# Convolution ahead of the context's norm, one scan quarter's stacks moved to transfers, later entry of two attention loops' last rows, and four more products ahead of the router's transposes

## What is computed

```
x = ln(x + mamba_block(x))            # ln, projection, depthwise conv of 3, selective scan, gate, small FFN
x = ln(x + cross_attention_0(x, ctx)) # 16 heads of 64, rotary keys, clipped logits
x = ln(x + moe_0(x))                  # 8 experts, top 2, GELU
x = ln(x + self_attention_1(x))       # 16 heads of 8, rotary                    ("a" below)
x = ln(x + cross_attention_1(x, ctx)) # 16 heads of 8, with a mask               ("x" below)
x = ln(x + moe_1(x))                  # 32 experts of 64, grouped top 6 of sigmoid scores, relu^2, one shared expert
# the scan of the first block, per channel d and state n:
#   delta = softplus(xc @ dt_w + dt_b);  h = exp(delta * A) * h + (delta * xc) * B;  y = sum_n h * C + D * xc
```

## Time and profile before

| | us |
|---|---|
| median of 3 runs | 506.44 (505.37 to 507.49) |
| profiled execution, its own time | 506.76 |
| its span in the profile | 505.0 |
| time outside the span | 1.76 |
| PE busy | 423.4 (84%) |
| DVE busy | 310.4 (61%) |
| ACT busy | 203.9 (40%) |
| chain that ended last: on PE | 56% |
| chain that ended last: on DVE | 27% |

### The profile page before, as it was taken

How to read it: one execution, slowest core, us unless ns; L and a number is a source line. 1 busy time by engine, 2 the same in 40 slices (tenths; PEclk the granted TensorE clock), 3 DMA queues, 4 the chain that set the end, 5 groups by cost and what they waited for, 6 DMA issues and landing times.

```text
span 505.0 us, 7196 instructions
## 1 busy us (share of the span) xinstructions
PE 423.4 (84%) x2724; PEld 256.2 (51%) x2732; DVE 310.4 (61%) x733; ACT 203.9 (40%) x259; POOL 142.2 (28%) x133
## 2 busy tenths in 40 slices
PE   0538989999999998799998867896768999979794
PEld 0207645444454466657668554445324455564493
DVE  4669976866777764325113689734996773237564
ACT  0565633233333331143333397670334445517400
POOL 3204656787767765101203000002000000014301
PEclk9868999999999999899999899899789999979898
DMA  8601000000023110600431500000000000010000
GB/s 299 246 19 55 1 2 1 1 1 1 0 75 135 42 43 14 228 16 25 92 46 29 74 13 2 3 2 1 1 1 2 1 3 3 1 31 2 0 1 21
DMA packets 7360, 19.37 MB, mean 38 GB/s; under 512 B 1751, under 2 KB 3127, under 8 KB 6807
## 3 DMA queue, kind: packets, MB, share of 16 engines
q1 hardware_dynamic: 7324, 18.91, 12.6%
HBM read 17.26 MB, written 1.15 MB: 36 GB/s over the span
## 4 chain that ended last, share of the span: by engine, by line
PE 56%; DVE 27%; issue 6%; POOL 5%; ACT 5%; DMA 1%; another core or an unknown queue 0%; DVEq 0%; POOLq 0%
PE ps L1228 53%; DVE ps L1081 4%; DVE mx_a L1085 2%; DVE ps L889 2%; DVE big L894 2%; POOL rstd L498 2%; POOL big L561 1%; ACT big L724 1%; DVE stats L797 1%; PE ps L1240 1%; PE ps L1601 1%; DVE big L966 1%; POOL big L568 1%; DVE normed L807 1%; DVE mid L825 1%
## 5 line engine op out<-in xcount | busy, mean ns | idle before, releaser
L1228 PE MATMUL ps<-big,late 128*32 128x256 f32 (+4 forms) x792 | 100.3, 381 | 11.3 <-DVE mx_x L1081 3.8
L1228 PE MATMUL ps<-late,big 128*128 128x128 f32 (+1 forms) x448 | 64.9, 277 | 3.4 <-DVE mx_x L1081 1.8
L750 ACT ACTIVATE big<-ps 128x1024 f32<-128x1024 f32 x48 | 48.9, 1024 | 39.3 <-PE ps L1228 39.0
L1228 PEld LDWEIGHTS ps<-big,late 128*32 128x32 f32 (+3 forms) x800 | 37.9, 115 | 51.1 <-issue 22.6
L496 POOL TENSOR_SCALAR vareps<-meanvar 128x4 f32<-128x4 f32 (+1 forms) x9 | 2.1, 231 | 212.1 <-DVE meanvar L800 212.1
L688 ACT ACTIVATE big<-ps 128x1024 f32<-128x1024 f32 x32 | 32.8, 1025 | 65.2 <-PE ps L1228 58.9
L1228 PEld LDWEIGHTS ps<-late,big 128*128 128x128 f32 (+1 forms) x448 | 45.0, 152 | 27.3 <-issue 20.6
L1081 DVE CUSTOM_DVE_ANT_0 ps<-ps,big 128x512 f32<-128x512 f32 x64 | 42.6, 716 | 10.5 <-PE ps L1228 7.5
L561 POOL TENSOR_TENSOR big<-big 128x512 f32<-128x512 f32 x32 | 41.0, 1283 | 28.1 <-DVE big L966 28.1
L966 DVE TENSOR_SCALAR big<-big 128x1024 f32<-128x1024 f32 x32 | 27.6, 863 | 33.3 <-ACT big L688 33.3
L1228 PE MATMUL ps<-ctx_r,attn_w 128*128 128x512 f32 x64 | 32.6, 618 | 0.7 <-ACT late L655 0.7
(11 more groups left out here) (246 smaller groups left out, 692.7 us busy)
## 6 DMA issues: line engine op xcount, KB each, us to landing
attn_w<-in_w_x SPq DMA_DIRECT2D x1, 2560.0 KB, 13.1
big<-parts_kx SPq DMA_DIRECT2D x18, 128.0 KB
late<-in_w_up SPq DMA_DIRECT2D x1, 2048.0 KB, 7.5
late<-in_w_dn SPq DMA_DIRECT2D x4, 512.0 KB, 3.8
attn_w<-in_w_up SPq DMA_DIRECT2D x1, 1024.0 KB, 7.1
attn_w<-in_w_dn SPq DMA_DIRECT2D x1, 1024.0 KB, 9.1
parts_kx<-ctx_r SPq DMA_DIRECT2D x1, 768.0 KB, 3.2
rowv<-in_rowv SPq DMA_DIRECT2D x1, 576.0 KB, 3.9
```

The lines of the kernel that those rows point to most:

```text
L750: nc.scalar.activation(ex1[:, n % 3, :].rearrange("p (r n) -> p r n", r=2), ps[:, 2 * (n % 2):2 * (n % 2) + 2, :], ACT.Exp, scale=scale).t ...
L1228: return nc.tensor.matmul(o, lhsT, rhs, start=start, stop=stop, skip_group_check=shared)
```

## The change

- ACT loads its first table before it waits for xT. DVE takes the context's statistics, then the convolution, then normalises the context. PE transposes the context behind the products for delta, B and C. POOL's residual sum waits for the context's norm.
- |z| is read by ACT straight from PSUM. ACT loads the exp table behind Silu, and computes A (`negA`) behind the context's evictions.
- PE gets 20, 10 and 20 idle products in the opening.
- Quarter 1's stacks are made by 6 further DMAs in place of DVE's 6 copies. The DMAs are issued by quarter (1, 2, 3), delta then delta*x in each. `ORDER`, `SUMMED` and the places of `y_of` (steps 7, 9, 14) follow.
- In both attentions the last two rows of the first stretch go to banks 6 and 7, and logits(0) waits for all rows but these two. `AHEAD["x"]` goes from 29 to 24. The spreads stand earlier. The exp table is loaded ahead of "a".
- `EARLY` goes from 12 to 16.

```diff
-        ORDER = ([(q, i) for two in ((0, 1), (2, 3)) for i in range(2) for q in two]
+        ORDER = ([(0, 0), (0, 1), (1, 0), (1, 1), (2, 0), (3, 0), (2, 1), (3, 1)]
                  + [(q, i) for i in (2, 3) for q in range(4)])
-        SUMMED = ((0, 1, 4, 5), (2, 3, 6, 7), (8, 9, 10, 11), (12, 13, 14, 15))
+        SUMMED = ((0, 2, 4, 5), (1, 3, 6, 7), (8, 9, 10, 11), (12, 13, 14, 15))
-        AHEAD = {"a": 24, "x": 29}
+        AHEAD = {"a": 24, "x": 24}
...
-            return ([(None, s, i % 4) for i, s in enumerate(first_slots(L))]
+            first = first_slots(L)
+            banks = [i % 4 for i in range(len(first) - 2)] + [6, 7]
+            return ([(None, s, bank) for s, bank in zip(first, banks)]
                     + [(n, s, 6 + i % 2) for i, (n, s) in enumerate(later)])
...  SP
-            for kind, parts in enumerate(("delta_parts", "dx_parts")):
-                for q in (2, 3):
+            for q in (1, 2, 3):
+                for kind, parts in enumerate(("delta_parts", "dx_parts")):
                     for i in range(PARTS):
...
-                                     ).then_inc(S["late_quads"], 16)
+                                     ).then_inc(S["second_quads" if q == 1 else "late_quads"], 16)
...  POOL
-            pool.wait_ge(ld["x"], 16)
+            pool.wait_ge(norm_out, normed_tiles("ctx"))
...
-                    pool.wait_ge(S["y_ps"], 1 if s < 10 else 2)
+                    pool.wait_ge(S["y_ps"], 1 if s == 8 else 2)
...  ACT
+            act.wait_ge(consts, 1)
+            set_table(ACT.Identity)
             to_cols(xT[:], 0, "xT_ps", "xT_done", v("ln_g"), v("ln_b"), 1)
...
+            set_table(ACT.Exp)
+            act.wait_ge(S["dt_ps"], 1)
+            nc.scalar.activation(dtmp[:, 0, :], ps[:, 3, :], ACT.Abs, bias=v("dt_b")
+                                 ).then_inc(S["z_done"], 1)
             act.wait_ge(S["z_done"], 1)
-            link(nc.scalar.activation(dtmp[:, 0, :], cv[:, 1, :], ACT.Abs))
...
+            set_table(ACT.Exp)
             act.wait_ge(ld["sel_s"], 32)
...  DVE: quad() is called for quarter 0 alone
-            quad(1, 0, "dx_quads")
-            quad(0, 1, "delta_quads")
-            quad(1, 1, "dx_quads")
+            quad(1)
...  PE
             pe.wait_ge(ld["ident"], 16)
+            idle_work(3, 20)
...
+            idle_work(3, 10)
             pe.wait_ge(S["xc_done"], 1)
...
+            idle_work(2, 20)
...
-                if s in (8, 10, 14):
+                if s in (7, 9, 14):
...
-                        return range(4) if m < 0 else [4 + m // 2] if m % 2 and 4 + m // 2 < 16 else []
-                    return [0] if m < 0 else [1 + m // 4] if m % 4 == 1 and 1 + m // 4 < 8 else []
+                        return range(5) if m < 0 else [5 + m // 2] if m % 2 and 5 + m // 2 < 16 else []
+                    return [0] if m < 0 else [1 + m // 3] if m % 3 == 1 and 1 + m // 3 < 8 else []
...
+                    if slot == ("row", AHEAD[L] - 2):
+                        pe.wait_ge(S[f"{L}_spread"], len(SPREADS[L]))
...
-                pe.wait_ge(S[f"{L}_redmax"], AHEAD[L])
-                pe.wait_ge(S[f"{L}_spread"], len(SPREADS[L]))
+                pe.wait_ge(S[f"{L}_redmax"], AHEAD[L] - 2)
...
-            EARLY = 12
+            EARLY = 16
```

More of the change, by code:

```diff
@@ L364, in before_in_bank @@
             at = [s for _, s, _ in placed].index(slot)
-            same = [s for n, s, bank in placed[:at]
-                    if bank == placed[at][2] and (n is None) == (placed[at][0] is None)]
+            same = [s for n, s, bank in placed[:at] if bank == placed[at][2]]
             return same[-1] if same else None
@@ L641, in _ @@
                         v("ctx_g"), v("ctx_b"), i + 1)
+            link(nc.scalar.activation(nA[:, 0, :], vec[:, VEC["A_log"][0]:VEC["A_log"][0] + NG],
+                                      ACT.Exp))
+            nc.scalar.mul(nA[:, 1, :], nA[:, 0, :], -1.0).then_inc(S["negA"], 1)
             act.wait_ge(S["negA"], 1)
@@ L843, in _ @@
             dve.wait_ge(ld["cx"], 16)
-            layernorm("ctx", cx, cx)
+            k_ctx = NORMS.index("ctx")
+            for j in range(NC_TILES):
+                ins = nc.vector.bn_stats(stats[:, j, :], cx[:, j, :])
+            link(ins)
+            for j in range(NC_TILES):
+                ins = nc.vector.bn_aggr(meanvar[:, k_ctx, j, :], stats[:, j, :])
+            ins.then_inc(norm_var, 1)
+            dve.wait_ge(norm_var, k_ctx + 1)
             dve.wait_ge(ld["vec"], 16)
@@ L853, in _ @@
                                            ALU.mult, ALU.add).then_inc(S["conv_done"], 1)
+            dve.wait_ge(norm_rstd, k_ctx + 1)
+            for j in range(NC_TILES):
+                nc.vector.tensor_scalar(cx[:, j, :], cx[:, j, :], meanvar[:, k_ctx, j, 0:1],
+                                        rstd[:, k_ctx, j:j + 1], ALU.subtract, ALU.mult
+                                        ).then_inc(norm_out, 1)
+            dve.wait_ge(norm_out, normed_tiles("ctx"))
             dve.wait_ge(ld["rope0"], 16)
@@ L866, in _, with quad @@
                   S["delta_parts"])
-            def quad(kind, q, done):
+            def quad(kind):
                 for i in range(PARTS):
-                    ins = nc.vector.tensor_copy(quads[32 * i:32 * i + 32, kind, q, :],
-                                                dparts[32 * q:32 * q + 32, kind, i, :])
-                ins.then_inc(S[done], 1)
+                    ins = nc.vector.tensor_copy(quads[32 * i:32 * i + 32, kind, 0, :],
+                                                dparts[0:32, kind, i, :])
+                ins.then_inc(S["first_quads"], 1)
             dve.wait_ge(S["delta_parts"], PARTS)
-            quad(0, 0, "delta_quads")
+            quad(0)
             dve.wait_ge(S["xc_done"], 1)
@@ L1257, in _ @@
             mm(ps[:, 2, :], w_mix[:, 1, :], xT[:]).then_inc(S["v1_ps"], 1)
-            pe.wait_ge(norm_out, normed_tiles("ctx"))
-            for i in range(2):
-                to_cols(6 + i, cx[:, 4 * i:4 * i + 4, :], "cxnT_ps")
+            idle_work(3, 10)
             pe.wait_ge(S["xc_done"], 1)
@@ L1264, in _ @@
             mm(ps[:, 5, :], w_mix[:, 4, :], xc[:]).then_inc(S["BC_ps"], 1)
+            pe.wait_ge(norm_out, normed_tiles("ctx"))
+            for i in range(2):
+                to_cols(6 + i, cx[:, 4 * i:4 * i + 4, :], "cxnT_ps")
+            idle_work(2, 20)
             pe.wait_ge(ld["sel"], 32)
@@ L1300, in _ @@
                     pe.wait_ge(S["dA_done"], s - 1)
-                if s < 2:
-                    pe.wait_ge(S["delta_quads"], s + 1)
+                if s == 0:
+                    pe.wait_ge(S["first_quads"], 1)
+                elif s == 2:
+                    pe.wait_ge(S["second_quads"], 16 * 2 * PARTS)
                 elif s == 4:
@@ L1305, in _ @@
                 mm(ps[:, s % 2, :], sel_g[:, i, :], quads[:, 0, q, :]).then_inc(S["spread_d"], 1)
[L1306 to L1307 removed]
+                if s == 0:
+                    pe.wait_ge(S["first_quads"], 2)
                 if s >= 2:
@@ L1311, in _ @@
                    ).then_inc(S["spread_x"], 1)
-                if s in (8, 10, 14):
-                    y_of((8, 10, 14).index(s))
+                if s in (7, 9, 14):
+                    y_of((7, 9, 14).index(s))
                 if s == 0:
```

11 lines of the change are left out of this document (2 added, 9 removed).

## The result

The changed kernel takes 493.5 us (median of 6 runs, 493.04 to 494.9) where the kernel before takes 506.97 on the same chip (505.11 to 510.05): a ratio of 0.973, with a 95% interval of 0.969 to 0.977. The forecast was 493.6. The profiled execution of the changed kernel has a span of 493.1 and took 494.9, so it lies 1.4 above its own median; 11.9 of span were gained where the working had 12.8.

What follows compares the result with a forecast made beforehand. PE was busy 84% of the span, but the chain of waits lay 56% on PE, 27% on DVE, so limits vary by stage. 7.6 - 1.3 - 0.4 + 0 + 3.5 + 3.4 = 12.8 gave 493.6 us, range 490.0 to 498.0.

Steps and rivals of the forecast that it cites:

- The opening: Start to the first multiplication by B: new order and idle products bring it to 32.65 from 40.26; gain 7.6 us.
- The rival that the idle products do not raise the clock: Opening: PE stays at the lower clock despite idle products; 3.8 us less gain, 497.4 us in all, chance 0.13.
- The late stacks: Early scan: more DMAs in SP's queue make step 4 wait for its stacks until 41.4; loss 1.3 us (0.5 to 2.5).
- The earlier y sum: Scan step 9: PE waits for POOL's product of step 7 ahead of y_of; loss 0.4 us (0 to 0.8).
- "a": Attention stage a: DVE enters its gapless stretch at the same time with two rows more; gain 0 (-0.7 to +1.2).
- "x": Attention stage x: earlier loop entry and cheaper max slots, less added loop rows and clock; gain 3.5 us (1.0 to 5.0).
- The term of -1.4: Entry of x's loop: PE, idle about 2.5 us before, runs some 2.8 us at the lower clock; cost 1.4 us.
- The last block: Router to first expert piece: the piece comes at 475.5 in place of 478.88; gain 3.4 us (2.4 to 4.4).
- the rival in which everything hides: Full clock entering x (+1.4), a gains two rows (+1.2), POOL's squares stop nothing (+1.0): 490.0 us, chance 0.07.
- The slower rivals: Loop of x: the clock falls at entry and stays down; some 550 us, or 522 for half, chance 0.02.

Runs made afterwards that it cites:

- the stacks by kinds: Changed kernel plus 17 idle products ahead of delta*x's spread, and SP issuing all nine delta stack DMAs before all nine of delta*x: 490.22 us, one execution.
- the y sums: Changed kernel with the first two sums of y put back behind the spreads of steps 8 and 10: steps 4 to 15 take 20.33 us.

## Where the prediction was right, and where not

**The opening** was right step by step: 7.54 for 7.6, with no milestone of the chain off by more than 0.3. The first idle group is worth 0.94 where 0.9 stood. The rival that the idle products do not raise the clock fell in the trace itself (1.96 for four passes), and so did the half that it booked for the second group: xc's products are at full clock with the idle groups and without any.

**The late stacks** were right in size and in mechanism (41.4 worked out, 41.41 measured; with PE kept at full clock in steps 0 to 3, the DMAs still hold step 4, until 41.62 with the clock that falls in the wait). What the working missed is that steps 1 and 2 were slow too, because PE came back cold after 3.5 us; it took PE's idle products to end early enough and did not ask what the clock does after them. The two losses lie over each other, so the sum did not feel it. That both ended at the same instant was chance.

**The earlier y sum** was booked at step 9 with 0.4. It costs 0.57, most of it at step 8. The step that failed is the choice of which sum waits: I followed the second and not the first.

**"a"** was given 0 and lost 1.04, outside my bound of -0.7. The argument for 0 holds as far as shown: with the clock kept up, the same order takes 49.85 against 49.92; the 0.58 that the added products cost there and the 0.65 of the loop's entry at full clock, neither of them in the argument, about cancel. What failed is that the argument took the clock of this stretch from the one trace of before, where it read 1.00, although PE is thin there in either order; it fell for 10 us. I had booked such a fall at the entry of "x" and none here. Nor had I booked that the entry of this loop, cold before, would be at full clock. (DVE is not without a gap in this stretch, as I read it: before the change it has one of 1.02, ahead of row 4.)

**"x"** was given 3.5 and gained 4.23. Its parts: the entry 4.61 earlier (4.7 booked); five rows more in the loop against cheaper max slots, 0.99 shorter together (0.6 booked from -1.1 and +1.7); the clock at the entry, booked at -1.4, was not paid in this trace. The clock fell some 5 us before the entry, at 365.1, behind a wait of 0.99 ahead of the first max transposes, and was up again from 368.5. Then a stack for the last slot landed late and PE waited 0.87, which no other trace here shows; with its tail it took 1.37. Without it "x" gains 5.60, as in six other traces. The term of -1.4 was no bad one as an average: of the ten traces with "x" as changed, two entered at 0.50 and paid 2.97 and 3.9, and in a third the clock fell 1.0 after the entry, for 1.75. It was mis-sized in that it comes whole or not at all. Nor does PE's idle time ahead of the entry decide it: after 2.17 to 2.19 of it PE entered at 1.00 once (the run with `EARLY` at 12), at 0.50 twice, and with the fall just behind it once.

**The last block** was given 3.4 and gained 3.23. The first piece comes 4.96 after cmb (4.8 worked out). One sum of the router (0.94) and the copies (1.61 for 0.88) are stretched beside a square, as expected; that makes 1.26 of the block, a little more than the 1.0 of the rival in which everything hides.

**The whole.** 12.8 worked out, 11.9 measured in the profiled pair; the median came out at 493.5 against 493.6, which fits a late stack (1.37) in the profiled execution alone; the others were not traced. Two errors, -1.04 in "a" and +2.1 in a usual "x", stand against each other: that the median was hit to 0.1 is in part luck. The slower rivals have nothing for them: the loop of "x" was back at its usual 1.98 a step from its fourth step on even in the coldest trace.

The trace agrees with the Trainium skill, "SBUF — State Buffer", shared port pair, in more than the forecast used: with the squares cut to 8 columns, the stretch of every such DVE operation is gone. And what the Trainium skill, "TensorE: Matmul & The Clock Gate", HAM oscillation, says against a PE that waits again and again showed at a place where I had not applied it, the start of "a" (granted 0.50 from 290.0 to 300.3).

## What to carry to other kernels

A granted clock of 1.00 in one trace is no property of a stretch where PE is thin: look how busy PE is there, and book the fall as a risk with its price (here 1.1 to 1.7 in "a", 1.8 to 3.9 at the entry of "x"), at every such place and not only at the one that the change touches. Idle products in the gaps kept it up over these rows, but count their passes against the gap (a float32 product is two), since each one too many holds up what stands behind it. And compare the clock at both ends of a stage before its time is explained: a cold entry of the kernel before hid 0.65 of the loss in "a". Two losses that end at the same instant hide each other: take both away in one run before calling either harmless.

## What the runs showed of the hardware

The clock did not need idle products to rise in the opening: without them it reads 1.00 from the end of the four slow passes of w1 and v1 (14.27 to 18.02). Nor did it in "x", in the changed kernel ahead of the loop, where it rose at 368.53 with PE busy for 1.67 of the 2 us before 368 and 0.78 of the 2 us from there:

```profile
368.00:370.00 2.00, 0.78 (x2) 0.13 (x2) 2.00 (x7) 0.10 (x1) 0.00 (x0) 0.87 0.02 4
```

The same instructions at the same place can find either clock. Four products between the scan and "a", touched by no edit, in the changed kernel and then in the run with the stacks by kinds:

```profile
200.00 2.52 PE L1243 MATMUL ps<-ctx_r,w_x 128*128 128x512 f32 x4
```

```profile
197.34 1.88 PE L1243 MATMUL ps<-ctx_r,w_x 128*128 128x512 f32 x4
```

The stretch from the last multiplication by B to "a" takes 224.8 and 224.9 in two of the thirteen traces behind the change, and 225.8 to 226.6 in the others and before it. The two (the stacks by kinds, and the y sums) are the only ones in which the clock does not fall here; in all others it falls 134.3 to 136.8 after that multiplication. Of the 1.57 between the two traces above, 0.92 lie in the eight products just ahead of this place (2.08 and 1.16) and 0.64 in these four. Why it falls in one execution and not in the next stays open. So a single execution of this kernel says little on an edit worth under 2 us; the stretches of its trace say more.
